# Self-attention's first steps: an early key bound for two groups, a row copied by the sync queue, ring slots 0 and 1 in another place

## What is computed

```python
pos_bias = jnp.einsum('ijf,hf->hij', table[idx], Wpos)
logits = jnp.einsum('bihd,bjhd->bhij', q, k) * scale + pos_bias[None]
attn = jax.nn.softmax(logits, axis=-1)
out = jnp.einsum('bhij,bjhd->bihd', attn, v).reshape(B, S, D)
x = _layernorm(x + jnp.einsum('bsd,ed->bse', out, Wout))
```

## Time and profile before

| what | value |
|---|---|
| median of 3 runs | 1292.52 us (1292.45 to 1293.67) |
| profiled execution, its own time | 1297.87 us |
| span of that execution | 1296.0 us |
| busy: TensorE, VectorE, ScalarE, GpSimd | 1180.9, 859.6, 794.3, 772.5 us |
| front | up to about 128 us |
| self-attention | from 129.6 to 612.9 us |
| mean granted clock of TensorE | 0.956 |

### The profile page before, as it was taken

The page is one execution under the profiler, slowest core; times in us unless marked ns, Lnnn a source line. Parts: engine busy times, 40 slices in busy tenths (PEclk is TensorE's granted clock), DMA queues, the critical chain, the costliest instruction groups (busy, mean ns, idle before and its releaser), DMA issues.

```text
span 1296.0 us, 28185 instructions
## 1 busy us (share of the span) xinstructions
PE 1180.9 (91%) x10747; PEld 683.0 (53%) x10747; DVE 859.6 (66%) x1468; ACT 794.3 (61%) x947; POOL 772.5 (60%) x515
## 2 busy tenths in 40 slices
PE   7998899999999999999899999539999999999980
PEld 3444233333333333333345453329999999999980
DVE  4454899999889998997547887724444444444445
ACT  4554899999999999998366667302222222222224
POOL 1233688788887888887246887734445444444433
PEclk9999899999999999999799999669999999999995
DMA  7699554495559554462267862977777777777748
GB/s 224 201 326 285 221 75 75 76 264 91 87 86 271 84 83 75 80 128 78 82 170 193 207 189 99 177 245 234 236 245 235 235 236 244 242 240 244 236 111 263
DMA packets 134207, 232.50 MB, mean 179 GB/s; under 512 B 31601, under 2 KB 80534, under 8 KB 133750
## 3 DMA queue, kind: packets, MB, share of 16 engines
q1 hardware_dynamic: 102416, 178.08, 46.9%
q0 software_dynamic: 25024, 39.74, 16.4%
q10 hardware_dynamic: 6630, 12.82, 3.5%
HBM read 103.91 MB, written 52.76 MB: 121 GB/s over the span
## 4 chain that ended last, share of the span: by engine, by line
PE 67%; DVE 15%; issue 5%; POOL 5%; ACT 5%; DMA 3%; ACTq 0%; SPq 0%; DVEq 0%; POOLq 0%
PE xp_ps_h L2371 20%; PE xp_ps_y L2383 9%; PE sa_sum L668 9%; PE sa_o L682 9%; DVE sa_probs L714 8%; PE sa_factor L668 4%; PE qp_ps L302 4%; PE qp_ps L329 2%; POOL sorted L1086 2%; ACT sa_probs L738 1%; PE xp_ps_x L2360 1%; DVE sa_o_out L702 1%; PE cb_misc L1240 1%; ACT fi_rows L2497 1%; PE cb_l L1255 1%
## 5 line engine op out<-in xcount | busy, mean ns | idle before, releaser
L714 DVE TENSOR_TENSOR sa_probs<-sa_sum,sa_strips 128x1024 f32<-128x1024 f32 x352 | 413.2, 1219 | 45.5 <-PE sa_sum L668 43.4
L758 POOL TENSOR_TENSOR sa_probs<-sa_probs,sa_factors 128x1024 f32<-128x1024 f32 x160 | 383.7, 2398 | 99.0 <-ACT sa_probs L732 99.0
L738 ACT ACTIVATE sa_probs<-sa_probs 128x1024 f32<-128x1024 f32 (+1 forms) x256 | 343.0, 1385 | 0.2 <-DVE sa_probs L714 0.2
L2371 PEld LDWEIGHTS xp_ps_h<-arena,big 128*128 128x128 f32 x2272 | 266.3, 193 | 5.1 <-ACT arena L2401 1.6
L2371 PE MATMUL xp_ps_h<-arena,big 128*128 128x128 f32 x2272 | 266.9, 276 | 0.9 <-ACT arena L2401 0.9
L682 PE MATMUL sa_o<-sa_probs,sa_v 128*17 128x512 f32 x2048 | 265.6, 594 | 0.8 <-POOL sa_probs L758 0.6
L2339 POOL DMA_INDIRECT y_sum<-stage,xp_place_of x71 | 113.1, 1593 | 192.2 <-DMA y_sum<-stage,xp_place_of 96.2
L668 PE MATMUL sa_sum<-sa_qk 97*32 97x512 bf16 x2816 | 201.6, 382 | 16.1 <-DVE sa_probs L714 7.0
L668 PEld LDWEIGHTS sa_sum<-sa_qk 97*32 97x32 bf16 x2816 | 63.2, 95 | 234.2 <-DVE sa_probs L714 130.9
L732 ACT ACTIVATE sa_probs<-sa_factor 128x1024 f32<-128x1024 f32 x160 | 164.5, 1028 | 4.9 <-PE sa_factor L668 3.4
L2383 PE MATMUL xp_ps_y<-big,arena 128*128 x568 | 134.5, 380 | 1.3 <-DVE arena L2438 1.3
(11 more groups left out here) (238 smaller groups left out, 1283.7 us busy)
## 6 DMA issues: line engine op xcount, KB each, us to landing
big<-big SPq DMA_DIRECT2D x142, 512.0 KB
sa_strips<-line SPq DMA_DIRECT2D x3, 3840.0 KB, 18.8
sa_qk<-qstack SPq DMA_DIRECT2D x84, 128.0 KB
sa_qk<-kstack SPq DMA_DIRECT2D x84, 128.0 KB
oT<-sa_o_out SPq DMA_DIRECT2D x32, 256.0 KB, 2.4
kstack<-qp_parts SPq DMA_DIRECT2D x48, 128.0 KB, 3.9
qstack<-qp_parts SPq DMA_DIRECT2D x48, 128.0 KB
sa_factors<-factor_line SPq DMA_DIRECT2D x3, 1920.0 KB, 23.1
```

Source lines behind the costliest of these rows:

```text
L714: nc.vector.tensor_tensor(probs[s % RING][:, 2 * half:2 * half + 2, :], ps_sum[sums_before(s, half) % 2][:, :, :], strips[hg % 2][:, 2 * h ...
L738: nc.scalar.activation(probs[s % RING][:, 0:heads, :], probs[s % RING][:, 0:heads, :], ACT.Exp, scale=0.25).then_inc(exp_done, 1)
L758: nc.gpsimd.tensor_tensor(probs[s % RING][:, 2:4, :], probs[s % RING][:, 2:4, :], factors[hg % 2][:, :, c1 - CH:c1][:, :, ::-1], ALU.mult) ...
L2371: last = nc.tensor.matmul(ps_h[parity % 2][:, n, m * P:(m + 1) * P], w_now[s % WRING][:, n, k, m * P:(m + 1) * P], xT[parity % 2][:, k, :] ...
```

## The change

- A second, early bound is made of the peaks of chunks 0 to 3, that is of batch entries 0 and 1: a reduce on VectorE in chunk 4, two more spare fills with their drains (`early_top` in chunk 5, `early_shift` in chunk 6), a power on GpSimd after chunk 6.
- `early_rows` writes row 96 of both key buffers with it in chunk 7, between `subtract(7, 1)` and `key_peak(7, 0)` on VectorE. The final bound is written once, as 1024 elements, into `shift_row`, and SyncE's queue copies it into row 96 when it loads m = 2 and m = 3.
- Steps 0 and 1 no longer wait for `front_stored`; they wait for `factor_stored` (chunk 2). Step 2 waits for it, on VectorE, ScalarE and GpSimd. TensorE waits for the banks that it takes over: the sum banks for `bound_done` 5 and for the last squares and subtractions, the factor bank for the last copy of values.
- `onehot` and `line`, used last in chunk 2, move to where ring slots 0 and 1 then lie; the ring is allocated ahead of the strips.
- An activation of one column (`warm`) stands ahead of ScalarE's first wait.
- The semaphore `bound_done` takes the place of `kmax_done`, counted to 7 instead of 4.

The diff, with less context:

```diff
@@ -134,6 +134,8 @@
         "front_stored": sem("front_stored"), "keys_shifted": sem("keys_shifted"), "pv_done": sem("pv_done"),
+        "shift_row": sb("shift_row", [P, S], BF16), "warm": sb("warm", [P, 1]), "bound_done": sem("bound_done"), "v_copied": sem("v_copied"),
+        "rest_done": sem("rest_done"), "sq_done": sem("sq_done"), "factor_stored": sem("factor_stored"),
         "o_copied": sem("o_copied"), "o_stored": [sem(f"o_stored{i}") for i in range(2)],
@@ -142,10 +144,11 @@
 SPARE = ("mix", "table", "line0", "line1", "line2", "line3", "keys0", "keys1", "gram0", "gram1", "values0", "values1",
-         "image0", "image1", "norm0", "norm1", "top", "shift")
+         "image0", "image1", "norm0", "norm1", "top", "early_top", "shift", "early_shift")
 SPARE_IN = {(0, 0): ("mix",), (0, 1): ("table",), (1, 0): ("line0", "line1"), (1, 1): ("line2", "line3"), (2, 0): ("keys0", "keys1"),
             (2, 1): ("gram0", "gram1"), (3, 0): ("values0", "values1"), (3, 1): ("image0", "image1"),
-            (4, 0): ("norm0", "norm1"), (5, 0): ("top",), (6, 0): ("shift",)}
+            (4, 0): ("norm0", "norm1"), (5, 0): ("top", "early_top"), (6, 0): ("shift", "early_shift")}
+EARLY_CHUNKS = 4
@@ -169,13 +172,13 @@
         k_top = sb("k_top", [P, 4])
+        k_early = sb("k_early", [P, 5])
         coeffs = sb("coeffs", [NF, TAPS])
...
         ramp = sb("ramp", [TAPS, RES])
-        onehot = sb("onehot", [RES, 2 * S])
+        onehot, line = cs["onehot"], cs["line"]
         combined = sb("combined", [TAPS, H])
         table = sb("table", [RES, H])
-        line = sb("line", [H, 2 * S])
         factor_rows = onehot[0:H, :]
@@ -184,15 +187,16 @@
-        hi_done, sq_done, rest_done, mid_done, lo_done = (
-            sem(n) for n in ("hi_done", "sq_done", "rest_done", "mid_done", "lo_done"))
-        root_done, peak_done, v_copied = sem("root_done"), sem("peak_done"), sem("v_copied")
+        hi_done, mid_done, lo_done = (sem(n) for n in ("hi_done", "mid_done", "lo_done"))
+        root_done, peak_done = sem("root_done"), sem("peak_done")
+        sq_done, rest_done, v_copied, factor_stored, bound_done = (
+            sa[n] for n in ("sq_done", "rest_done", "v_copied", "factor_stored", "bound_done"))
-        kmax_mm, kmax_done, shift_set = sem("kmax_mm"), sem("kmax_done"), sem("shift_set")
+        kmax_mm, shift_set = sem("kmax_mm"), sem("shift_set")
@@ -289,6 +293,12 @@
                     last = nc.tensor.matmul(out[0:1, 0:P], cs["top"][:, 0:1], cc["ident"][:, :], start=True, stop=True)
+                elif kind == "early_top":
+                    pe.wait_ge(bound_done, 1)
+                    last = nc.tensor.matmul(out[0:1, 0:8], k_early[0:8, 0:1], cc["ident"][0:8, 0:8], start=True, stop=True)
+                elif kind == "early_shift":
+                    pe.wait_ge(spare_drained, use["early_top"] + 1)
+                    last = nc.tensor.matmul(out[:, 0:1], cc["ones"][0:1, :], k_early[0:1, 1:2], start=True, stop=True)
                 else:
@@ -331,14 +341,14 @@
             def key_bound():
-                pe.wait_ge(kmax_done, 1)
+                pe.wait_ge(bound_done, 3)
                 pe.wait_ge(sq_done, 4 * (NCH - 1) + 2)
...
             def spread_bound():
-                pe.wait_ge(kmax_done, 2)
+                pe.wait_ge(bound_done, 4)
                 nc.tensor.matmul(ps_u[1][:, 0:1], cc["ones"][0:1, :], k_top[0:1, 1:2], start=True, stop=True
@@ -431,7 +441,7 @@
             act.wait_ge(kmax_mm, 2)
-            nc.scalar.activation(k_top[:, 2:3], ps_u[1][:, 0:1], ACT.Sqrt).then_inc(kmax_done, 1)
+            nc.scalar.activation(k_top[:, 2:3], ps_u[1][:, 0:1], ACT.Sqrt).then_inc(bound_done, 1)
@@ -475,6 +485,10 @@
                     last = nc.vector.reduce_max(cs["top"][0:1, 1:2], bank[0:1, 0:P], AXX)
+                elif kind == "early_top":
+                    last = nc.vector.reduce_max(k_early[0:1, 1:2], bank[0:1, 0:8], AXX)
+                elif kind == "early_shift":
+                    last = nc.vector.tensor_copy(k_early[:, 2:3], bank[:, 0:1])
                 else:
@@ -515,20 +529,38 @@
+            def early_bound():
+                dve.wait_ge(peak_done, 2 * EARLY_CHUNKS)
+                nc.vector.reduce_max(k_early[0:8, 0:1], k_peak[:, 0:2 * EARLY_CHUNKS], AXX).then_inc(bound_done, 1)
+
+            def early_rows():
+                dve.wait_ge(set_up, 4)
+                nc.vector.tensor_scalar(k_early[:, 4:5], k_early[:, 3:4], -1.05, None, ALU.mult).then_inc(bound_done, 1)
+                dve.wait_ge(bound_done, 2)
+                dve.wait_ge(shift_set, 1)
+                for i in range(2):
+                    nc.vector.tensor_scalar(sa["k"][i][ROWS:ROWS + 1, :, :].rearrange("p h s -> p (h s)"),
+                                            ones_row[ROWS:ROWS + 1, :], k_early[ROWS:ROWS + 1, 4:5], None, ALU.mult
+                                            ).then_inc(sa["keys_shifted"], 1)
+
             for c in range(NCH):
...
                 subtract(c, 1)
+                if c == NCH - 1:
+                    early_rows()
                 key_peak(c, 0)
...
                     dve.wait_ge(peak_done, 2 * NCH)
-                    nc.vector.reduce_max(k_top[0:8, 0:1], k_peak[:, :], AXX).then_inc(kmax_done, 1)
+                    nc.vector.reduce_max(k_top[0:8, 0:1], k_peak[:, :], AXX).then_inc(bound_done, 1)
                 subtract(c, 3)
+                if c == EARLY_CHUNKS:
+                    early_bound()
                 if c == 3:
@@ -536,16 +568,14 @@
                     dve.wait_ge(kmax_mm, 1)
-                    nc.vector.reduce_max(k_top[0:1, 1:2], ps_u[0][0:1, 0:8], AXX).then_inc(kmax_done, 1)
+                    nc.vector.reduce_max(k_top[0:1, 1:2], ps_u[0][0:1, 0:8], AXX).then_inc(bound_done, 1)
                 for n in range(2):
                     copy_values(c, n)
-            dve.wait_ge(kmax_done, 3)
-            nc.vector.tensor_scalar(k_top[:, 3:4], k_top[:, 2:3], -1.05, None, ALU.mult).then_inc(kmax_done, 1)
-            dve.wait_ge(kmax_done, 4)
-            dve.wait_ge(shift_set, 1)
-            for i in range(2):
-                nc.vector.tensor_scalar(sa["k"][i][ROWS:ROWS + 1, :, :].rearrange("p h s -> p (h s)"), ones_row[ROWS:ROWS + 1, :],
-                                        k_top[ROWS:ROWS + 1, 3:4], None, ALU.mult).then_inc(sa["keys_shifted"], 1)
+            dve.wait_ge(bound_done, 5)
+            nc.vector.tensor_scalar(k_top[:, 3:4], k_top[:, 2:3], -1.05, None, ALU.mult).then_inc(bound_done, 1)
+            dve.wait_ge(bound_done, 6)
+            nc.vector.tensor_scalar(sa["shift_row"][ROWS:ROWS + 1, :], ones_row[ROWS:ROWS + 1, 0:S], k_top[ROWS:ROWS + 1, 3:4],
+                                    None, ALU.mult).then_inc(bound_done, 1)
@@ -558,6 +588,9 @@
                                             ).then_inc(set_up, 1)
+                    pool.wait_ge(spare_drained, use["early_shift"] + 1)
+                    nc.gpsimd.tensor_tensor(k_early[:, 3:4], k_early[:, 2:3], cs["half"][:, :], ALU.pow
+                                            ).then_inc(set_up, 1)
@@ -592,9 +625,9 @@
         strips_loaded, factors_loaded = sa["strips_loaded"], sa["factors_loaded"]
+        probs = [sb(f"probs{i}", [P, HPG, CH]) for i in range(RING)]
         strips = [sa["strips"], sb("strips1", [P, HPG, STRIP])]
         factors = [sa["factors"], sb("factors1", [P, 2, STRIP])]
-        probs = [sb(f"probs{i}", [P, HPG, CH]) for i in range(RING)]
         o_out = sa["o_out"] = [sb(f"o_out{i}", [P, CH]) for i in range(2)]
@@ -611,6 +644,9 @@
                 load_keys(sp, io, sa, m)
+                if m < 4:
+                    sp.dma_start(k[m % 2][ROWS:ROWS + 1, :, :],
+                                 sa["shift_row"][ROWS:ROWS + 1, :].unsqueeze(1).to_broadcast([1, HPG, S])).then_inc(keys_shifted, 16)
                 load_values(sp, io, sa, m)
@@ -619,7 +655,7 @@
-            sp.wait_ge(keys_shifted, 2)
+            sp.wait_ge(sa["bound_done"], 7)
             load_bias(1)
@@ -649,16 +685,23 @@
                     pe.wait_ge(loaded[m % 2], HEAD_LOADS * (m // 2 + 1))
-                    if m < 2:
-                        pe.wait_ge(keys_shifted, m + 1)
+                    if m < 4:
+                        pe.wait_ge(keys_shifted, (1, 2, 2 + 16, 2 + 32)[m])
                 for half in range(2):
...
                         into, ready = ps_factor, factor_scores
+                        if factors_before(s) == 0:
+                            pe.wait_ge(sa["v_copied"], 2 * NCH)
                         if factors_before(s) >= 1:
...
                         into, ready = ps_sum[n % 2], sum_scores
+                        if n == 0:
+                            pe.wait_ge(sa["bound_done"], 5)
+                        elif n == 1:
+                            pe.wait_ge(sa["sq_done"], 4 * NCH)
+                            pe.wait_ge(sa["rest_done"], 4 * NCH)
                         if n >= 2:
@@ -693,7 +736,7 @@
```

(13 more changed lines are left out.)

2 lines of the change are left out of this document (1 added, 1 removed).

## The result

Changed kernel: 1291.67 us median of 20 runs (1289.22 to 1299.03). Kernel before on the same chip: 1295.81 us (1292.45 to 1301.34). Ratio 0.9972, 95% interval 0.9959 to 0.9985: 3.6 us (0.28%) faster, by 1.9 to 5.3 us (the two medians alone lie 4.1 us apart). The forecast started from 1292.52 us, the median of three runs, which is 3.3 us under that of the twenty; so the difference is compared, and not 1290.0 with 1291.67. My 2.5 us lie within the interval, but I had given "no difference to be measured" the larger chance, and the two profiled executions show another course than the one I forecast.

What follows compares the result with a forecast made beforehand. Self-attention runs at ScalarE's pace, so only its start can be shortened. With D of 1.28 and 1.6 us behind the last copy, the first addition moves by -2.5 us: 1292.52 - 2.5 = 1290.0 us, range 1288.2 to 1292.1.

Steps and rivals of the forecast that it cites:

- the later stages' own drift: Behind self-attention: one of the forecast's small terms, which together gave it a span of 1289.2 to 1290.9 us.
- The front longer by D: Front, before self-attention: added matmul pairs, key rows and GpSimd's hold lengthen it by 1.28 us, between 0.1 and 1.6.
- The two small pairs: TensorE, chunks 5 and 6: early_top and early_shift lengthen the front by 0.43 us, bounds 0 and 0.62.
- their excess over the cover: VectorE, chunk 7: two key rows of 2.67 us exceed 2.46 us of free time by about 0.15 us.
- GpSimd's hold: VectorE, chunk 7: GpSimd's running subtraction delays the first key row by 0.7 us, bounds 0 and 0.92.
- Behind the last copy: VectorE, after the last copy of values: small tensor_scalar, row of 1024 and clearing take 1.6 us before the first addition.
- Store, step 2: Self-attention's start: the last store lands at 134.73, so the wait moved to step 2 costs nothing; bounds 0 and 2.2 us.
- row copies: SyncE's queue, m = 2 and 3: one more issue of 0.4 us ahead of the values' load, price 0.
- ring: Buffer placement: slots 0 and 1 trade places with two other buffers, no instruction changes in shape, price 0.
- stays up: Self-attention's start: rival that shorter TensorE pauses keep its clock up, winning 1.5 us more: 1288.5 us, chance 0.15.
- comes later: Self-attention's start: rival that the slow clock falls in the filled pipeline, costing 3.2 instead of 1.5: 1291.7 us, chance 0.14.
- the shift: VectorE's first addition in self-attention: moves from 133.45 to 130.95, that is -2.5 us.

Runs made afterwards that it cites:

- after_6: One of seven profiled executions of the unchanged changed kernel: no low clock in the front, first addition at 130.96, last output copy at 609.6, span 1287.1 us.
- late_row: Changed kernel with the second key row written after the final bound's last reduce instead of ahead of key_peak(7, 0): ratio 0.9969 to the kernel before.
- after_filled: Changed kernel with dummy matmuls in TensorE's pauses in chunk 7 and around step 1's scores, both rows left in place: 1289.24 us, ratio 0.9970 to the kernel before.
- before_4: Kernel before, unchanged, fourth look: timed ratio 0.9998; its profile has 6.8 us of low clock in the front and a span of 1291.8 us.
- filled: Changed kernel with the second key row moved as in late_row, plus dummy matmuls in TensorE's pauses: 1300.56 us, ratio 0.9943 to the kernel before.
- after_4: Changed kernel, unchanged, fourth look: 1292.51 us, ratio 0.9993 to the kernel before; profiled span 1289.5 us.
- after: First profiled execution of the changed kernel, unchanged: 6.8 us of low clock in the front, first addition at 133.90, span 1289.9 us.
- before_filled: Kernel before with dummy matmuls in TensorE's gaps in chunk 7 and around step 1's scores: 1291.82 us, ratio 0.9984 to the kernel before.

## Why the prediction was right, and where it failed

**Which steps failed.** I set "no difference to be measured" at 0.49 and "faster" at 0.44, and the kernel is faster beyond the interval. The term behind that call is "the later stages' own drift", which I counted as a few tenths of a microsecond, from no row. The runs showed 2.1 of the 3.3 us between the mean spans behind self-attention, and all 6.1 us of the first pair's. The noise was also less than I took: I set faster at 2.6 us and more, and the twenty runs told 1.7 (the measurements of twelve runs 2.3 to 3.1). With 1.7, nearly all of the forecast's own span would have been "faster".

In the mechanism another step failed: the sum took the front's last matmuls at full speed and so put the clock there at nothing. The front's clock fell in 6 of 7 profiles, for up to 2.9 us, and in the same 6 the first addition came later than 131.5, my own sign of being wrong. In after_6, whose front kept its clock, the path that I forecast is the one that ran, from the first addition to the last output copy. That the time is near the forecast in spite of both is luck: the front's clock took from the gain about what the later stages gave.

**The front longer by D: right in the sum, not in its terms.** 1.16 us in the first pair (123.83 against 122.67) and again at `subtract(7, 2)` (122.31 against 121.15); forecast 1.28. The two small pairs took 0.15 of it and not 0.43. The norm in chunk 6 had waited 0.43 us for ScalarE, and that wait swallowed most of them, as my bound of 0 had it; TensorE's timelines of before and after:

```profile
108.29 0.38 PE L312 MATMUL qp_norm<-qp_squares,qp_members 128*8 128x512 bf16 x1 [0.43 <-ACT qp_squares L425]
...
118.41 0.38 PE L312 MATMUL qp_norm<-qp_squares,qp_members 128*8 128x512 bf16 x1
```
```profile
108.44 0.38 PE L322 MATMUL qp_norm<-qp_squares,qp_members 128*8 128x512 bf16 x1
...
118.56 0.38 PE L322 MATMUL qp_norm<-qp_squares,qp_members 128*8 128x512 bf16 x1
```

The rows took the other 1.01 and not 0.85: their excess over the cover is 2.67 - 2.46 = 0.21 by the rows that I cited, where I wrote 0.15, and 0.29 in the trace. The rows take 3.21 instead of 2.49, so GpSimd's hold costs 0.72, forecast 0.70. The Trainium skill ("SBUF — State Buffer", section "Who interferes with whom") would make it the whole overlap, 0.92. The trace has 0.72: the mechanism agrees, the size is that of my own row.

**Behind the last copy: right.** 1.75 us in all seven, to 0.01, forecast 1.6; the row of 1024 took 0.48, not 0.35.

**Store, step 2, row copies, ring: right.** The store held step 2 in one of the seven profiles of the changed kernel (after_6), by 0.24 us, and ScalarE came behind its scores there. Step 32 starts with no idle time. SyncE issues the row in 0.66 us at 179.27, well ahead. With the moved waits put back no gain is measured (waits_back).

**The clock in the front.** I looked for it only at self-attention's start (rivals "stays up" and "comes later") and took the front's own matmuls at full speed in D. TensorE's pause ahead of the norm grew from 0.47 to 1.57 us, with another of 1.03 behind it, and I gave that no term but its length. In the profiles without fillers of kernels that hold the two added pairs, the clock fell in the front in 8 of 9 (the seven, waits_back and late_row); in the three with fillers in none; in the kernel before in 1 of 7. That the gaps bring the fall is what these counts suggest; which gap does it is not shown, since late_row fell with a pause of 0.48 us and after_filled did not with one of 1.14. A fall is worth up to 2.9 us, which the kernel before mostly hides under the store's wait (before_4) and the changed kernel passes on. I named the store's wait as the thing removed and did not ask what else it had been covering.

**The reference: the second, smaller miss.** I measured the shift from one profile with the first addition at 133.45. The mean of seven is 134.27, since the store's landing (4.96 to 6.33 us) and the front's own course both move. The shift without a fall is thus about 134.27 - 130.96 = 3.3 us, not 2.5; the second number is that of one execution.

**What remains of the gain.** On the means of the table: the front ends 3.3 us later (1.2 by D, the rest by the clock and the spread of starts), the way from there to the first addition is 4.1 us shorter, so the addition is 0.8 us earlier. The shorter low time at the start (7.3 against 11.7 us) adds 0.5: last copy 1.3 us earlier. The other 2.1 us of the spans' 3.3 arise behind it. There the low time from 615 to 665 is 6.4 us less and that behind 700 us 2.4 more, 4.0 less together. Fitting time against mean granted clock over the timed runs gives 1.03 to 1.19 us per 0.001 of clock, which is 0.40 to 0.46 us per us of low time, so 1.6 to 1.8 us for 4.0: the size fits. At equal clock the same fits put the changed kernel 1.4 +- 1.0, 2.4 +- 1.4 and 0.8 +- 0.8 us below the kernel before on the three chips, 1.5 on average, close to the 1.3 at the last copy.

**What stays open.** Whether the shorter low stretch near 622 us belongs to the change. For it: 10.2 us or less in 7 of 7, against 13.6 or more in 6 of 7. Against: filled and after_filled start self-attention early too and show 13.7, and no instruction there differs; waits_back, which holds the rest of the change and starts late, shows 13.7 as well. The timed runs speak for a link with the early start: the mean granted clock of the changed kernel is higher than that of the kernel before on all three chips, by 0.0020 +- 0.0014, 0.0032 +- 0.0017 and 0.0009 +- 0.0016, and that of waits_back is not, 0.0003 +- 0.0014. It isn't in the front and at self-attention's start that this arises, where the seven profiles have as much low time before as after. How the start would act so far on is not shown. Two windows of 4 us, before_4 and then after_4, show that the busy times are alike and the clock is low in one and not in the other:

```profile
622.00:626.00 4.00, 2.90 (x10) 1.33 (x12) 2.34 (x7) 1.41 (x2) 1.42 (x3) 0.54 0.74 215
```
```profile
622.00:626.00 4.00, 3.17 (x16) 1.20 (x16) 2.33 (x7) 1.54 (x3) 1.42 (x3) 1.00 0.77 196
```

So of the measured 3 to 3.6 us about 1.5 are the change at equal clock, by the fits on three chips. The rest goes with the clock; it comes with the change in the timed runs, by a way that stays open.

## What to carry to other kernels

A wait that is removed may have been covering more than the work you see: ask which variable things end under it (here the front's matmuls at half clock), since they become the start of the next stage. Before the difference of two profiles is explained, take several of each and compare the same landmark in all; here one landmark moves by 3 us between executions of one kernel. And a pause of TensorE of one or two microseconds in front of work that others wait for may be worth filling with idle matmuls, counted by their real length; here after_filled ran 3.3 us under after_4 by the medians, with an interval of 2.4 each way.

## What the runs showed of the hardware

- Two executions of one kernel (after and after_6), whose instructions on TensorE, VectorE and GpSimd start within 0.01 us of each other from 114.5 to 123.95, part at the clock: last eight value matmuls in 3.78 or 1.99 us. These starts don't tell which.
- The low time at the start is not less with the change, only placed otherwise: 1.0 + 11.7 us before, 5.3 + 7.3 after. In the front 6.8 us of it cost 2.9, and 2.5 of these stand in the two groups of eight value matmuls (2.73 and 3.78 us instead of 1.99 each).
- Once low, the clock isn't brought back at once by work. In before_filled it fell half a microsecond after a stretch (130 to 132) with 0.19 us of matmuls and stayed at 1.2 GHz for 17.1 us, through twelve fillers on end and the first steps.
- The store of 272 KB landed 4.96, 5.99, 5.93, 6.33, 5.83 and 5.13 us after its issue in the six executions where it released the first addition: a spread of 1.4 us in the start of self-attention. The prediction's sum had the shortest of these as its only value; 7.7 us stood in it as a bound. With the waits put back it landed in 4.08.
